# A drain behind TensorE's matmuls carries each signal, and GpSimd gathers the tiles that ScalarE fetched row by row

## The reference, cut to what matters

```
m_in = concatenate([x[src], x[dst], edge_attr], axis=-1)      # 64 + 64 + 16 features for each edge
h = silu(m_in @ W1 + b1)
messages = silu(h @ W2 + b2)
agg = segment_sum(messages, dst, num_segments=12500)
u = silu(concatenate([x, agg], axis=-1) @ W3 + b3)
out = layernorm(x + u)
```

## Time and profile before

| | |
|---|---|
| times of the runs | 4520.94, 4534.21, 4543.54 us (median 4534.21) |
| span of the profiled execution | 4497.7 us; its own time is not listed apart, the median of the runs is 36.5 us above its span |
| TensorE matmul busy | 3654.5 us, 81% |
| TensorE weight loads | 2747.4 us, 61% |
| VectorE busy | 2757.0 us, 61% |
| ScalarE busy | 1046.2 us, 23% (starting DMAs is not counted) |
| GpSimd busy | 2591.6 us, 58% |
| mean granted clock of TensorE | 0.918 |
| DMA | 16 engines busy about a tenth of the span |

### The profile page before, as it was taken

How to read it: one execution, slowest core, us unless ns; L and a number is a source line. 1 busy time by engine, 2 the same in 40 slices (tenths; PEclk the granted TensorE clock), 3 DMA queues, 4 the chain that set the end, 5 groups by cost and what they waited for, 6 DMA issues and landing times. The chain is left out here.

```text
span 4497.7 us, 68074 instructions
## 1 busy us (share of the span) xinstructions
PE 3654.5 (81%) x19180; PEld 2747.4 (61%) x19180; DVE 2757.0 (61%) x4834; ACT 1046.2 (23%) x1714; POOL 2591.6 (58%) x2754
## 2 busy tenths in 40 slices
PE   1588888888888888888888888888888888888888
PEld 1366666666666666666666666666666666666665
DVE  2366666666666666666666666665665666666667
ACT  0222222222222222222222222222222222222223
POOL 7365655556555655656555555555555555555650
PEclk6789999999999999999999999999999999999998
DMA  4211111111111111111111111111111111111110
GB/s 100 59 29 34 32 28 34 33 34 29 34 33 28 34 34 30 32 28 39 28 34 28 35 32 28 33 33 33 28 33 34 28 33 28 34 32 28 38 23 11
DMA packets 335197, 150.34 MB, mean 33 GB/s; under 512 B 224958, under 2 KB 290527, under 8 KB 334822
## 3 DMA queue, kind: packets, MB, share of 16 engines
q0 software_dynamic: 87808, 90.09, 9.5%
q1 hardware_dynamic: 237238, 54.50, 5.7%
q10 hardware_dynamic: 9776, 1.37, 0.2%
HBM read 136.10 MB, written 9.62 MB: 32 GB/s over the span
## 5 line engine op out<-in xcount | busy, mean ns | idle before, releaser
L547 POOL DMA_INDIRECT edge_in<-in_x_dram,src_i x2744 | 2590.4, 944 | 1789.7 <-issue 743.5
L1165 PE MATMUL pick_ps<-parts,rows_T 128*128 128x512 f32 (+1 forms) x9100 | 2298.7, 405 | 564.0 <-issue 268.6
L1165 PEld LDWEIGHTS pick_ps<-parts,rows_T 128*128 128x128 f32 x9100 | 1698.8, 196 | 993.7 <-issue 384.4
L646 ACT ACTIVATE z_ps<-z_ps,zero_col 128x512 f32<-128x512 f32 x391 | 258.9, 662 | 2859.1 <-DVE z_ps L855 1975.8
L855 DVE TENSOR_TENSOR z_ps<-z_ps,b_rep 128x512 f32<-128x512 f32 x391 | 272.4, 697 | 920.9 <-remote 553.3
L1099 PEld LDWEIGHTS in_ps<-ident,edge_in 128*128 128x128 f32 x3128 | 347.7, 144 | 362.1 <-issue 341.6
L1126 PEld LDWEIGHTS z_ps<-w_bd,h_T 128*128 128x128 f32 x3128 | 471.4, 219 | 145.6 <-DVE pair L878 82.8
L1126 PE MATMUL z_ps<-w_bd,h_T 128*128 128x128 f32 x3128 | 485.7, 306 | 81.0 <-DVE pair L878 61.1
L1120 PE MATMUL z_ps<-in_T,w_in 128*64 128x512 f32 x782 | 441.2, 646 | 19.8 <-issue 14.1
L1099 PE MATMUL in_ps<-ident,edge_in 128*128 128x128 f32 x3128 | 442.4, 286 | 13.9 <-issue 7.7
L1121 PE MATMUL z_ps<-in_T,w_in 128*64 128x512 f32 x782 | 442.4, 649 | 8.6 <-issue 8.5
(11 more groups left out here) (104 smaller groups left out, 1231.5 us busy)
## 6 DMA issues: line engine op xcount, KB each, us to landing
edge_in<-in_x_dram ACTq DMA_DIRECT2D x3968, 0.2 KB
edge_in<-in_x_dram,src_i POOLq DMA_INDIRECT x2744
ea<-in_edge_attr_dram SPq DMA_DIRECT2D x48, 512.0 KB
w_in<-node_terms SPq DMA_DIRECT2D x391, 12.0 KB
node_terms<-h_T SPq DMA_DIRECT2D x12, 256.0 KB
node_terms<-lot_T SPq DMA_DIRECT2D x12, 256.0 KB
y<-in_x_dram SPq DMA_DIRECT2D x15, 192.0 KB
term<-node_terms SPq DMA_DIRECT2D x15, 192.0 KB
```

Source lines behind the costliest of these rows:

```text
L547: pool.indirect_dma_start(out=edge_in[:, to_slot, t, XS], out_offset=None, in_=x[:, :], in_offset=bass.IndirectOffsetOnAxis(ap=indices[:, ...
L1165: last = nc.tensor.matmul(pick_ps[at % PICK_BANKS][:, 0:(b - a) * H], rows_T[:, n % ROW_SETS, c, :], parts[:, j, a:b, :].rearrange("p k f ...
```

## The change

Each of the six signals that TensorE gives in the loop (`s_in_T`, `s_z1`, `s_z2`, `s_keys`, `s_agg`, `s_round`) was an increment on the last matmul of its group. It becomes an increment on a drain that follows this matmul: an instruction that ends when everything before it on TensorE has ended. The fetch by rows goes: its index loads on SyncE, its registers, loads and DMAs on ScalarE, its waits on TensorE. GpSimd gathers those tiles, one more in each group that had one. The order of everything else stays.

```diff
     def tiles_of(g):
-        return TT if g == FULL else T - picked(g) - fetched(g)
+        return TT if g == FULL else T - picked(g)
...
-                    if k * B + u in ROWS_OF:
-                        load_row_indices(ROWS_OF[k * B + u])
...
-                for part, ahead in enumerate(FETCH):
-                    if fetched(g + ahead):
-                        fetch_rows(g + ahead, part)
                 second_silu(0, g + 1)
...
-                if fetched(v):
-                    j, before = fetch_of(v)
-                    for odd in range(2):
-                        pe.wait_ge(s_fetched[j][odd], (before + 1) * (P // 2 * 16))
-                transpose_tiles(v % S).then_inc(s_in_T, 1)
+                transpose_tiles(v % S)
+                pe.drain().then_inc(s_in_T, 1)
...
-                nc.tensor.matmul(z1_ps[H:P, :], w_in[:, v % NW, :], in_T[:, 1, :], start=True, stop=True).then_inc(s_z1, 1)
+                nc.tensor.matmul(z1_ps[H:P, :], w_in[:, v % NW, :], in_T[:, 1, :], start=True, stop=True)
+                pe.drain().then_inc(s_z1, 1)
...
-                by_edges().then_inc(s_z2, 1)
+                by_edges()
+                pe.drain().then_inc(s_z2, 1)
...
-                                 ident_r[:, :], start=True, stop=True).then_inc(s_keys, 1)
+                                 ident_r[:, :], start=True, stop=True)
+                pe.drain().then_inc(s_keys, 1)
...
-                last.then_inc(s_agg, 1)
+                pe.drain().then_inc(s_agg, 1)
...
                 if done_with:
-                    last.then_inc(s_round, 1)
+                    pe.drain().then_inc(s_round, 1)
```

More of the change, by code:

```diff
@@ L200, in gnn_layer @@
         base_bc = sb("base_bc", [P, Q * P])
-        row_i = sb("row_i", [1, 2, P], I32)
         base_i = sb("base_i", [1, Q * P], I32)
@@ L274, in gnn_layer @@
         s_ea = [sem(f"ea_loaded{q}") for q in range(RING)]
-        s_row_i = [sem(f"row_indices_loaded{j}") for j in range(2)]
-        s_fetched = [[sem(f"rows_fetched{j}_{o}") for o in range(2)] for j in range(2)]
         s_tail = sem("tail_src_loaded")
@@ L377, in ring @@
             return v // CH % RING, v % CH
-        def fetch_of(g):
-            n = g // S - 2
-            return n % 2, n // 2
         def loaded(k, v):
@@ L447, in store_lot @@
                 sp.dma_start(out[bass.ds(b * LN, LN), :].rearrange("(k p) f -> p k f", p=P), y[:, 0:LT, :]).then_inc(lots.out, 16)
[L449 to L453, removed]
             def body(k, with_lot=True, last=False):
@@ L662, in deviation @@
                 nc.scalar.activation(tables[:, :], zero_col[:, :], ACT.Silu, bias=zero_col[:, :])
[L664 to L674, removed]
             def step(g):
@@ L701, in redo @@
                     deviation(lots, b + first, LT)
-            row_regs = [act.alloc_register(f"row{i}") for i in range(ROWS)]
             with act.If(general == 0):
@@ L1147, in sum_messages @@
                 for i, tile in ((0, 0), (1, TT - 1 if tail else T - 1)):
-                    last = nc.tensor.matmul(agg_ps[i * H:(i + 1) * H, OH], pair[:, v % 2, i, :], edge_in[:, v % S, tile, OH],
-                                            start=True, stop=True)
-                last.then_inc(s_agg, 1)
+                    nc.tensor.matmul(agg_ps[i * H:(i + 1) * H, OH], pair[:, v % 2, i, :], edge_in[:, v % S, tile, OH],
+                                     start=True, stop=True)
+                pe.drain().then_inc(s_agg, 1)
             def pick_piece(n, piece):
@@ L1164, in pick_piece @@
                 for j in range(PARTS):
-                    last = nc.tensor.matmul(pick_ps[at % PICK_BANKS][:, 0:(b - a) * H], rows_T[:, n % ROW_SETS, c, :],
-                                            parts[:, j, a:b, :].rearrange("p k f -> p (k f)"),
-                                            start=(c == 0 and j == 0), stop=(done_with and j == PARTS - 1))
+                    nc.tensor.matmul(pick_ps[at % PICK_BANKS][:, 0:(b - a) * H], rows_T[:, n % ROW_SETS, c, :],
+                                     parts[:, j, a:b, :].rearrange("p k f -> p (k f)"),
+                                     start=(c == 0 and j == 0), stop=(done_with and j == PARTS - 1))
                 if done_with:
-                    last.then_inc(s_round, 1)
+                    pe.drain().then_inc(s_round, 1)
             def pieces(g):
```

## The result

| | before | after |
|---|---|---|
| median of the runs | 4534.21 us | 5707.68 us |
| lowest and highest | 4520.94, 4543.54 | 5687.66, 5721.19 |
| span of the profiled execution | 4497.7 us | 5685.8 us (the run of 5687.66) |
| TensorE matmul busy | 3654.5 us | 4417.3 us |
| mean granted clock | 0.918 | 0.847 |

The ratio is 1.2597 (95% interval 1.2563 to 1.2631): 26% slower, where 4.5% faster was forecast and 4850 us was the end of the range. The groups by line of the kernel after (columns as in the earlier trace rows) and its waits are read first.

A forecast was written before the change was run, and what follows sets the result against it. TensorE's steps were taken to be stretched by signals late during GpSimd's gathers. 173.6 us start, 3199 + 62 of steps, 836 of drains and 19 of end gave 4290 span, plus 36.5: 4330 us, 4.5% faster; range 3700 to 4850.

The forecast's parts named there:

- What bounds the kernel: TensorE's steps: signals on matmuls come out late while GpSimd gathers, losing 2.6 us a step, about 1,000 us.
- the prediction's sum without drains: Span with prompt signals and free drains: start, 379 steps of 8.44 us, 12 others and end, 3454 us.
- The fetch: Dropping 3,968 small DMAs from ScalarE's queue and 31 index loads from SyncE's: value 0, bounds -100 to 0 us.
- The gathers: 31 more tiles gathered on GpSimd at 1.25 us each: hidden, or 39 us if its bursts still set the period.
- The price of a drain: On TensorE, 2,614 drains at 0.32 us each for tail, restart and sequencer: 836 us, bounds 405 to 1,700.
- The third piece: A drain instruction's own way through TensorE's sequencer, shown by no row: taken as 0.07 us, at most 0.40.
- The sum: 173.6 before the loop, 3199 + 62 of steps, 836 of drains, 19 of end: 4290 us span, 4330 us time.
- One range: Prompt signals with drains of 0.24 to 0.38 us: 4080 to 4490 us, chance 0.47.
- The gain: Drain signals come when matmuls end, so TensorE's steps cost 8.44 us instead of 11.04.
- the quiet stretch: Stretch near the end where GpSimd gathers nothing: signals prompt, steps of 8.44 us, taken as the model for the gain.
- Drains only add: Rival: late release is something drains don't touch, so their 836 us adds to 4534: 5370 us; 0.17 with its harder form.
- its harder form: Drains can't end before the delay clears, so TensorE stands for the rest of each burst: 18.4 us a step, 7,400 us.

The follow-up runs named there:

- the later condition: Four later occasions on four chips, every TensorE signal prompt: the unchanged kernel took 3467 to 3468 us, the changed kernel once more 4334.18 us, ratio 1.2502.
- the drained kernel: Kernel with all six drains, signals prompt: 4339.8 us with the fetch kept (drains alone against the kernel before, ratio 1.2515), 4334.18 us with its tiles gathered.
- the later run: The changed kernel run once more, unaltered, beside the kernel before on the same chip: 4334.18 us against 3467.32, ratio 1.2502.

## Why the prediction was wrong

With four traces, two kernels in two conditions, the 1,188 us between the spans of the first measurement can be taken apart.

| us | before | after | difference |
|---|---|---|---|
| span in the later condition | 3465.7 | 4330.9 | 865 |
| more TensorE busy in the first one (lower clock, same matmuls) | 3654.5 - 3338.9 = 316 | 4417.3 - 3775.4 = 642 | 326 |
| the rest: more waiting in the first one | 716 | 713 | -3 |
| span in the first measurement | 4497.7 | 5685.8 | 1188 |

The 638 us of holding and 87 us ahead of the loop (the first drain behind transposes starts at 166.8 us against 80.0, in the rows above) are about the 713 of the kernel after. The kernel before has the same 87 us among its 716; by the timelines the rest are waits that start with a late signal.

**What bounds the kernel: half right.** That TensorE lost some 1,000 us with late signals fits what came later: with prompt signals the kernel before has a span of 3465.7, and the prediction's sum without drains was 3454. That the two are so near is partly luck: the first second layer starts at 87.2 us, not 173.6, and the steps take 3446.7 - 87.2 = 3359.5 us, not 3261. That gathers by themselves make signals late was wrong: they run as densely later with signals at 0.04 us. But in the first trace the tie is close, as its semaphore updates show, set against the ends of the matmuls. Of 267 groups of transposes that ended in a burst of gathers, one had its signal within 0.1 us, and the median was 3.1 us; of the 122 others 69 had. And nine in ten of the transposes' late signals (over 0.6 us) came out 1.5 to 2.1 us after the end of a gather. So gathers look like one part, and a condition that the later runs lack is the other: the lateness is not the kernel's alone.

**The fetch: right.** Worth nothing in the drained kernel, where signals are prompt: 4334.18 with its tiles gathered, 4339.8 with the fetch.

**The gathers: right where drained.** Hidden there; 37 us where TensorE has no drains.

**The price of a drain: right.** Forecast 0.32 us, 836 in all; measured 0.334, 872, with prompt signals. The third piece, which had no row, was taken as 0.07 and is 0.084.

**The sum: right for another starting point.** In the later condition the changed kernel took 4334 us, and 4330 was forecast; but it is a loss of 25% there, since the kernel before takes 3467, and the nearness is partly luck. The part before the loop is 87.4 us and not 173.6, the loop is 4311.0 - 87.4 = 4223.6 us and not 3261 + 836 = 4097, and the 36.5 us from span to time are 1.8 in the later runs. One range doesn't follow from its own working: drains of 0.24 us give 3454 + 627 + 36.5 = 4118, not 4080.

**The gain: this step failed.** "If a drain's signal comes when the matmuls end, the consumers start as in the quiet stretch." In the first measurement a drain did not end when its matmuls did: the drains were held for 638 us in all, most of it behind the window, and the waiting is 713 us where it was 716 without drains. It moved from the consumers to TensorE. (That the two sums are equal within 3 us may be chance.) The 4497.7 - 3454 = 1,044 us that prompt signals were to bring did not come, the price of the drains was paid on top, and the low clock cost TensorE twice as much, 642 us against 316: a clock above 0.95 was forecast, and 0.847 was measured. In the other condition there was nothing to gain. So the change loses either way, 25 or 26%.

**The rivals.** "Drains only add" had 0.17 with 5370 us and was the nearest; it lacked the lower clock, 326 us of the 338 that it missed by. Its picture, holes where no drain is, is not what the trace shows: the holes lie behind the drains. In its harder form TensorE would stand for the rest of each burst, 7,400 us; it stood for part of it, 638 / 391 = 1.6 us a step. The argument against it, that matmuls go on while signals are stuck, was sound for the array and said nothing of when a drain ends. The rule of the Trainium skill on this (PSUM — Partial Sum Buffer, Engine vs sequencer instructions), that an increment on the matmul fires at its completion, stood against the change. The later traces agree with it at 0.04 us; those of the first measurement do not, and there the drains behind the window and the second layer ended late as well.

**Open.** What made TensorE's signals late, and its drains long, in the first measurement. Gathers alone don't (the same in both conditions), nor does the number of small packets alone (tried where signals were prompt), nor the fetch (the first measurement has it in one kernel and not in the other). ScalarE's queue was slow in the same microseconds, which points to something outside TensorE that both share. One rival no run tests is the recording of the profile itself: both traces of the first measurement lack many semaphore updates (254 of the 350 of the keys are there in the kernel before, 162 in the kernel after), and the later ones have nearly all. The condition never came back, and so whether a drain is held by the same thing as a matmul's signal is read from one trace, not tried.

## What to carry to other kernels

A drain behind each group of matmuls costs TensorE about a third of a microsecond, because the tail of one group, the next weight load and the waits behind it no longer overlap; with nearly seven in a step of 8.6 us that is a quarter of the kernel, whoever carries the signal. Before a change is built to cure late signals, time the same program again on another chip: if the lateness goes away, the program alone doesn't make it. And two things that come and go together in one trace (bursts of gathers, stuck signals) are a guess at a cause until one of them is taken away where the trouble is seen: taken away where there is no trouble, it tells nothing.

## What the runs showed of the hardware

- A kernel's time was 4534 us in one measurement and 3467 on four other occasions, four chips, within 0.2% there. In the first one TensorE's signals came late, by 8 us in the worst case shown; the granted clock was 0.918 and is 0.993 to 0.996 in the later profiles.
- In the first measurement signals of transposes that ended in a burst of gathers were 3.1 us late in the median, and more than half of the others under 0.1 us; in the later traces the median is 0.014 us, gathers or not. So the lateness went with the gathers there, and with something that the later runs lack.
- With prompt signals a drain with nothing in flight costs 0.084 us; one behind matmuls 0.21 to 0.33, by what else overlaps it.
- Small holes (0.07 to 0.34 us, behind the drains) did not lower TensorE's clock (1.00 in the stretch below, of the changed kernel in the later run); the same kernel in the first measurement, with holes of 0.76 and 1.40 us in the step shown, ran at 0.85.

```profile
300.00:4150.00 3850.00, 3406.56 (x17318) 2393.99 (x17318) 2465.28 (x4288) 959.60 (x1493) 2373.50 (x2507) 1.00 0.16 32
```

```profile
300.00:5500.00 5200.00, 4141.86 (x17946) 2867.20 (x17946) 2547.34 (x4434) 994.57 (x1543) 2445.81 (x2582) 0.85 0.13 25
```
